# A decoder layer on one core: the output projection as one full-fp32 matmul, in place of three products of rounded halves

## The reference

```python
    q = hidden_states @ Wq                      # [16, 128, 1024]
    k, v = jnp.split(hidden_states @ Wkv, 2, axis=-1)
    # 16 heads of 64
    scores = jnp.einsum('bid,bjd->bij', q, k) * scale
    probs = jax.nn.softmax(scores, axis=2)
    out = jnp.einsum('bij,bjd->bid', probs, v)  # heads side by side: [16, 128, 1024]
    return out @ Wo + bo                        # Wo: [1024, 256]

x = _layernorm(x + attn(x)); x = _layernorm(x + xattn(x, ctx)); x = _layernorm(x + ffn(x))
```

## Time and profile before

| | us |
|---|---|
| median of 3 runs | 843.74 (843.56 to 845.28) |
| the profiled execution, device time | 843.9 |
| its span from the first to the last instruction | 842.1 |
| busy in it: PE | 734.7 (87%) |
| DVE | 472.6 (56%) |
| ACT | 330.7 (39%) |
| POOL | 238.2 (28%) |
| mean granted clock of TensorE | 0.914 |

### The profile page before, as it was taken

How to read it: one execution, slowest core, us unless ns; L and a number is a source line. 1 busy time by engine, 2 the same in 40 slices (tenths; PEclk the granted TensorE clock), 3 DMA queues, 4 the chain that set the end, 5 groups by cost and what they waited for, 6 DMA issues and landing times.

```text
span 842.1 us, 15192 instructions
## 1 busy us (share of the span) xinstructions
PE 734.7 (87%) x5072; PEld 628.2 (75%) x5073; DVE 472.6 (56%) x1079; ACT 330.7 (39%) x989; POOL 238.2 (28%) x193
## 2 busy tenths in 40 slices
PE   4798999998979979799679989999999999998762
PEld 4687787877868868588668878888888888786320
DVE  4334444665855667647678844555555555555354
ACT  4575666655655646546442202222222222221011
POOL 2200010101303104022145456076077000600672
PEclk9899999998989989989685899999999999999655
DMA  8266674001001010020142245145135211210242
GB/s 310 62 218 227 202 255 157 2 13 55 10 26 51 14 38 26 2 63 2 57 156 76 88 140 155 39 162 168 37 119 170 78 37 37 63 33 20 82 145 79
DMA packets 62509, 77.40 MB, mean 92 GB/s; under 512 B 5836, under 2 KB 54520, under 8 KB 62456
## 3 DMA queue, kind: packets, MB, share of 16 engines
q1 hardware_dynamic: 53832, 47.29, 17.4%
q0 software_dynamic: 8608, 29.37, 10.9%
q10 hardware_dynamic: 16, 0.01, 0.0%
HBM read 45.04 MB, written 31.62 MB: 91 GB/s over the span
## 4 chain that ended last, share of the span: by engine, by line
PE 63%; DVE 13%; ACT 9%; POOL 6%; issue 6%; DMA 2%; another core or an unknown queue 0%; POOLq 0%; SPq 0%; DVEq 0%; ACTq 0%
PE bank L954 13%; PE bank L707 8%; PE bank L709 6%; PE bank L708 6%; ACT arena L1061 5%; PE bank L924 4%; PE bank L926 4%; PE bank L925 4%; PE bank L934 4%; PE bank L864 3%; PE bank L827 3%; POOL arena L697 3%; POOL xg_dram L632 1%; ACT arena L1034 1%; PE bank L876 1%
## 5 line engine op out<-in xcount | busy, mean ns | idle before, releaser
L954 PE MATMUL bank<-w_ring,hidT_hi 128*128 x320 | 121.2, 412 | 3.3 <-DVE hidT_lo L1575 3.3
L1179 ACT ACTIVATE hidT_hi<-bank 128x512 fp32r<-128x512 f32 x80 | 43.5, 595 | 176.2 <-PE bank L934 176.2
L1061 ACT ACTIVATE arena<-bank,negmx 128x128 f32<-128x128 f32 x256 | 90.8, 375 | 3.4 <-DVE negmx L1216 2.7
L632 POOL DMA_INDIRECT xg_dram<-arena,slot x32 | 33.8, 1055 | 181.2 <-DVE slot L1415 173.5
L954 PE MATMUL bank<-w_ring,hidT_lo 128*128 x320 | 84.1, 283 | 0.0
L1548 DVE TENSOR_TENSOR arena<-bank,b_rep 128x512 f32<-128x512 f32 x80 | 55.3, 691 | 40.9 <-PE bank L926 40.5
L1554 DVE TENSOR_REDUCE work<-bank 128x256 f32<-128x512 f32 x40 | 27.7, 692 | 81.0 <-PE bank L954 81.0
L954 PEld LDWEIGHTS bank<-w_ring,hidT_hi 128*128 128x128 f32 x320 | 60.8, 190 | 15.2 <-issue 3.9
L924 PE MATMUL bank<-w_ring,xgT_hi 128*128 x160 | 67.4, 421 | 4.5 <-DVE xgT_lo L1567 2.8
L926 PE MATMUL bank<-w_ring,xgT_lo 128*128 x160 | 63.8, 399 | 0.0
L925 PE MATMUL bank<-w_ring,xgT_hi 128*128 x160 | 62.9, 393 | 0.0
(11 more groups left out here) (243 smaller groups left out, 1882.7 us busy)
## 6 DMA issues: line engine op xcount, KB each, us to landing
xg_dram<-zeros SPq DMA_DIRECT2D x9, 2176.0 KB, 9.3
w_raw<-in_L_ffn_W_dram POOLq DMA_DIRECT2D x16, 1024.0 KB, 6.3
work<-xg_dram SPq DMA_DIRECT2D x40, 128.0 KB, 2.1
y_dram<-work SPq DMA_DIRECT2D x40, 128.0 KB, 1.7
b_rep<-in_L_ffn_b_dram POOLq DMA_DIRECT2D x8, 512.0 KB
work<-gmax_dram SPq DMA_DIRECT2D x14, 256.0 KB, 3.6
arena<-in_x_dram SPq DMA_DIRECT2D x8, 256.0 KB, 2.7
xres<-in_x_dram SPq DMA_DIRECT2D x1, 2048.0 KB, 15.2
```

The lines of the kernel that those rows point to most:

```text
L954: last = pe.matmul(o, l, r, start=c == 0 and l is both[0], stop=c == FC - 1 and l is both[0])
L1061: last = nc.scalar.activation(probs[:, n % 2, h * S:(h + 1) * S], ps_score[:, h * S:(h + 1) * S], ACT.Exp, bias=negmx[:, n % 2, h:h + 1], ...
```

## The change

The three fp32r products of each chunk of the output projection become one full-fp32 matmul, with the sums and the weights as they are. `oT_hi` and `oT_lo` become one fp32 tile `oT`, which ACT fills with the same copy without rounding; DVE's `rest_o` goes, at all 32 places. The weights are loaded once into `wo_sb`, at the place of `wo_hi`, and POOL's rounding and subtraction go. What waited for the split waits for the copy (`oT_copied`) or the load (`wo_loaded`). The tile `wo_lo` is no longer allocated, so the tiles behind it lie 8 KB lower. No instruction moves against the others on any engine.

```diff
@@ tiles
-        wo_lo = sb("wo_lo", [P, IC, D], F32R)
+        wo_sb = arena[:, 3 * KC * INNER:3 * KC * INNER + IC * D].rearrange("p (c n) -> p c n", c=IC)
-        wo_raw = arena3[:, KC * INNER:KC * INNER + IC * D].rearrange("p (c n) -> p c n", c=IC)
-        oT_hi, oT_lo = (over(4 * at, base, name, 2 * IC * S)[:, :].rearrange("p (b c t) -> p b c t", b=2, c=IC)
-                        for at, base, name in ((off[0], arena2_at, "oT_hi"), (0, norms_at, "oT_lo")))
+        oT = arena2[:, off[0]:off[0] + 2 * IC * S].rearrange("p (b c t) -> p b c t", b=2, c=IC)
@@ SP
-            sp.dma_start(wo_raw, wo.rearrange("(c p) n -> p c n", p=P)).then_inc(wo_loaded, 16)
+            sp.dma_start(wo_sb, wo.rearrange("(c p) n -> p c n", p=P)).then_inc(wo_loaded, 16)
@@ POOL
-            pool.wait_ge(wo_loaded, 16)
-            pool.tensor_copy(wo_hi, wo_raw).then_inc(wo_rounded, 1)
-            pool.wait_ge(wo_rounded, 1)
-            pool.tensor_tensor(wo_lo[:, :, :], wo_raw, wo_hi.bitcast(F32), ALU.subtract).then_inc(wo_split, 1)
-            pool.wait_ge(wo_split, 1)
@@ PE, out_proj
-                pe.wait_ge(oT_split, i * STEPS + 2 * half + b + 1)
+                pe.wait_ge(oT_copied, i * STEPS + 2 * half + b + 1)
...
                 for c in range(4 * half, 4 * half + 4):
-                    last = three(ps_wo[:, 0:D], oT_hi[:, b, c, :], oT_lo[:, b, c, :],
-                                 wo_hi[:, c, :], wo_lo[:, c, :], c == 0, c == IC - 1)
+                    last = pe.matmul(ps_wo[:, 0:D], oT[:, b, c, :], wo_sb[:, c, :], start=c == 0, stop=c == IC - 1)
@@ PE, weighted_sums
-                    pe.wait_ge(oT_split, n)
+                    pe.wait_ge(oT_copied, n)
@@ PE, before the loop
-            pe.wait_ge(wo_split, 1)
+            pe.wait_ge(wo_loaded, 16)
@@ ACT
-                    nc.scalar.copy(oT_hi[:, b, 4 * half:4 * half + 4, :],
-                                   ps_oT.rearrange("p (c t) -> p c t", c=4)).then_inc(oT_rounded, 1)
+                    nc.scalar.copy(oT[:, b, 4 * half:4 * half + 4, :],
+                                   ps_oT.rearrange("p (c t) -> p c t", c=4)).then_inc(oT_copied, 1)
@@ DVE
-            def rest_o(n):
-
-                half, b = step(n % STEPS)
-                dve.wait_ge(oT_rounded, n + 1)
-                hi, lo = (t[:, b, 4 * half:4 * half + 4, :] for t in (oT_hi, oT_lo))
-                dve.tensor_tensor(lo, ps_oT.rearrange("p (c t) -> p c t", c=4), hi.bitcast(F32), ALU.subtract)\
-                    .then_inc(oT_split, 1)
...
-                    if n > 0:
-                        rest_o(n - 1)
                     if n + 1 < STEPS * PAIRS:
                         maxima(n + 1)
...
-            rest_o(STEPS * PAIRS - 1)
             both_norms(A)
```

More of the change, by code:

```diff
@@ L108, in decoder_layer @@
         wq_lo = sb("wq_lo", [P, KC, INNER], F32R)
-        wo_lo = sb("wo_lo", [P, IC, D], F32R)
         wkv_lo = over(0, w_raw_at, "wkv_lo", 2 * KC * INNER)[:, :].rearrange("p (c n) -> p c n", c=KC)
-        wq_hi, wkv_hi, wo_hi = (
+        wq_hi, wkv_hi = (
             over(4 * at, arena_at, name, n)[:, :].rearrange("p (c n) -> p c n", c=c)
-            for at, name, n, c in ((0, "wq_hi", KC * INNER, KC), (KC * INNER, "wkv_hi", 2 * KC * INNER, KC),
-                                   (3 * KC * INNER, "wo_hi", IC * D, IC)))
+            for at, name, n, c in ((0, "wq_hi", KC * INNER, KC), (KC * INNER, "wkv_hi", 2 * KC * INNER, KC)))
+        wo_sb = arena[:, 3 * KC * INNER:3 * KC * INNER + IC * D].rearrange("p (c n) -> p c n", c=IC)
         wq_raw = arena3[:, 0:KC * INNER].rearrange("p (c n) -> p c n", c=KC)
-        wo_raw = arena3[:, KC * INNER:KC * INNER + IC * D].rearrange("p (c n) -> p c n", c=IC)
         wk_raw = work[:, 0:KC * INNER].rearrange("p (c n) -> p c n", c=KC)
@@ L264, in decoder_layer @@
         attn_split = sem("attn_split")
-        wo_rounded = sem("wo_rounded")
-        wo_split = sem("wo_split")
         x_rounded = sem("x_rounded")
@@ L280, in decoder_layer @@
         oT_done = sem("oT_done")
-        oT_rounded = sem("oT_rounded")
-        oT_split = sem("oT_split")
+        oT_copied = sem("oT_copied")
         wo_done = sem("wo_done")
```

## The result

Thirteen runs of each kernel give a median of 846.38 us after the change (845.14 to 848.58) and 843.49 us before it (840.82 to 845.28). The ratio is 1.0042, with a 95% interval of 1.0029 to 1.0054. The change costs 2.9 us by the medians; the forecast was 9.2 us.

What follows compares the result with a forecast made beforehand. The chain is mostly PE, on it through the 28 output units of pairs 0 to 6. Units +8.4, last pair +1.1 and DVE -0.3 sum to +9.2 us on 843.7: 852.9 us, range 848.5 to 857.

Steps and rivals of the forecast that it cites:

- The step that failed: Attention stage: anything longer before a k unit delays ACT's copy of it and all behind equally; 28 units, +8.4 us.
- the clock could fall elsewhere: Turns shift about 1.2 us, so low-clock stretches may move: +-2 us, within range; clock worse by over 4 us 0.02.
- 28 units: Output projection units of pairs 0 to 6, all on PE's chain: +0.30 us each, +8.4 us, bounds 7.8 to 9.5.
- The four holes: PE's wait for ACT after step 1, about 4.2 us, low clock behind it; counted five times, forecast unchanged.
- the low stretches growing or vanishing: Sign that the forecast is wrong: stretches of low granted clock on PE grow or vanish in the changed kernel's profile.
- The rival of dear passes: Each fp32 pass costs as much as an fp32r product, a unit +0.48 us: 858.3 us; chance 0.08.
- The rival that PE is not the bound: DVE or ACT have slack at each step, so the longer units hide: 843.4 to 844 us; chance 0.02.
- The last pair: Its last two output units, on the chain after a 4.4 us PE wait: +1.1 us, bounds 0.6 to 1.7.
- The two units of step 3: Last pair, at half clock: +0.9 us each, +1.7 for both, hidden by the 4.4 us PE wait behind them.
- Two paths ending 0.03 us apart: End of the hole: DVE's subtraction and maxima against ACT's gate steps and copies; removing subtractions gains only 0.3 us.
- no 4.1 us came back: Rival of a full DVE saving: the maxima set the restart, six subtractions return 4.1 us: 849.1 us; chance 0.09.
- The rival of a kept clock: Hole closes enough for PE to keep its clock, about 3.4 us per turn, -17 against +9.5: 836 us; chance 0.03.

Runs made afterwards that it cites:

- the clean pair: Before and changed kernel, both with the same identity matmuls (17 per hole, 16 at other places, from the second turn): 847.82 and 856.27 us, against 841.84 for plain before.
- Filling the holes: Kernel before plus 16 identity matmuls in each PE hole from the fourth pair on: 831.72 us against 841.56, ratio 0.9891.
- the dense set: Kernel before with identity matmuls in each hole (17) and in front of step 1's and 2's transposes and step 2's k unit: 847.82 us against 841.84.
- the second run of before: Kernel before, unaltered, run again on the chip of the single-delay kernel for a trace: 839.76 us.

## Why the prediction was wrong

**The step that failed** is the one that carried the sum from the units to the end: anything longer in front of a k unit "moves that copy, and everything behind it, by the same amount". It does so with the clock held up: 7.69 us measured where 28 units less DVE were forecast at 8.1. It does not where low stretches lie on the way. I had written that the clock could fall elsewhere, and called it plus or minus 2 us, part of the range and centred on nothing. It is neither small nor centred: at the last turn it takes back 4.2 to 5.5 of 7.7 us. As long as work is added in front of a stretch that stays, the delay is spent partly in time that would have been slow.

The account, for the profiled runs on the first chip:

- 28 units, as the clean pair has them at the last turn's step 0: 7.7 (28 times 0.287 would be 8.0, so at most 0.35 us of it is DVE's).
- The short stretch at 142, gone: -1.8, from step 1 to step 2 of the third turn.
- The four holes, each from step 1's copy of the transposed weights to step 3's, against the same in the clean pair: -0.7, -0.8, -1.0 and -1.0, so -3.5.
- Small amounts elsewhere: -0.2. That leaves 2.2, and 2.2 is measured (388.04 - 36.17 against 386.17 - 36.48).
- From there to the last two units it falls to 1.7 (428.99 and 427.59, with the 0.31 us by which this run's first copy was earlier). The clean pair loses 0.6 as well, from 7.7 to 7.1 at the last copy; I haven't placed it.
- The last two units: +1.9. Together 3.6 us, less the 0.31 of the start: the work behind them starts 3.3 us later (435.80 and 432.50), and the execution ends 2.8 us later.

The forecast named the low stretches growing or vanishing as a sign that it would be wrong. Both came: one vanished at 142, and the one over the last two units grew.

**PE's price** was right: 0.287 per unit (1.15 us for the first four, by ACT's copies) against 0.30, from a row of the same shape in another stage. The rival of dear passes is out. The rival that PE is not the bound is out too, by the clean pair.

The page "FP8 and Floating Point Precision" of the Trainium skill (section TensorE Precision Notes) has four passes for true fp32. The trace has two records of 0.216 us each for a matmul, which agrees only if a record holds two passes.

**The last pair.** Its two units on the chain were forecast at +1.1 us with a bound of 1.7, and cost 1.9. The mix of clocks was carried over from before; after runs the first unit and over half of the second at the low clock, in a stretch that is 6.8 us long in place of 3.4. Why it is longer isn't shown. The wait in front of them was to fall from 4.4 to 2.7 us and stayed 4.4. The two units of step 3 were priced at +0.9 each; the first took 3.54 in place of 2.70, but the second 1.82 in place of 2.35, since the clock was back for it, so PE came to the wait 1.35 us later. The DVE read that ends the wait came 1.40 us later. It follows, without a pause, on work that POOL releases and not these units. What was to be hidden hardly arose.

**DVE.** Two paths ending 0.03 us apart were read rightly: no 4.1 us came back, and the wait of 4.15 for ACT is unchanged. The amount over the stage is at most 0.35 us with the clock up and 0.2 between the kernels with and without the subtractions; of the 2.1 us where they alone were taken out, 1.7 are a low stretch that fell away.

**The rival of a kept clock** was priced at 3.4 us a turn, with a fill of the hole as the condition, and counted five times. The rows have four waits of 4.1 to 4.2 us and one of 0.35 (at 138.99), so its 17 us should have been 13.6. Its place was right and its condition too narrow. It needs no shorter wait. Filling the holes gave 9.8 us with the wait turned into work. The clock is also what ate the cost of the change, by a part of each stretch; the forecast gave the rival 0.03 and looked only for the whole of it.

## What to carry to other kernels

When the granted clock falls in the same place of every turn, do not move its stretches along with the work when you add or remove something. Price the edit twice, once at full effect and once with what the stretches give back (here 0.8 us for a restart 1.0 us behind the start of one), and let the range hold both. Check at the first and the last turn whether the distance between stretches is the same as that between restarts; here 54.6 against 54.4 us gave away, before any run of the changed kernel, that they drift. To measure what an edit costs by itself, hold the clock up with the same fillers in both versions; and try the fillers for their own sake, since here they gain more (1.1%) than the change costs (0.4%). More of them need not be better: 17 in a hole won nothing over 16, and the dense set made before 0.7% slower. And note where the stretches lie before laying two traces side by side: two runs of the same kernel differ here by 0.5 to 0.8 us, as much as their stretches do.

## What the runs showed of the hardware

I had not expected the low stretches to have a length and a spacing of their own. In the traces of before, the changed kernel, the kernel with DVE's work put back and the one with added work, each of the four stretches behind a hole is 6.8 us long, and the next begins 54.6 us after it, whether the restarts are 54.3 or 54.7 us apart. From run to run the whole row moves: in the second run of before they begin at 191.2, 245.8, 300.4 and 355.0, that is 1.6 us earlier, in a run that started 1.1 us earlier. Nor do they stay put whatever the kernel does: without DVE's subtractions, where the work up to the first hole is 2.1 us early, the row begins 2.9 us earlier against the first copy than in before. What sets that place was not tried.

The fall needn't wait for the next matmul. In after the clock is down at 247.0 while PE still waits, up to 248.05. PE's first work behind the wait is then slow from its first record.
